# Eight experts' rows scattered to planes of their own, and added to the output on DVE

## What is computed

```
x_flat = layernorm(h).reshape(N, 128)                     # N = 4096
probs  = softmax(x_flat @ Wr, axis=0)
vals, idx = top_k(probs.T, 1024)                          # 8 experts x 1024 rows
g = gelu(x_flat[idx] @ W1[e] + b1[e])                     # 128 -> 512
out_e = g @ W2[e] + b2[e]                                 # 512 -> 128
output = zeros_like(x_flat).at[idx].add(vals * out_e)
result = h + output
```

## Time and profile before

| | |
|---|---|
| median of 3 runs | 872.06 us (868.32 to 873.8) |
| the profiled execution, its own time | 873.6 us |
| its span | 871.7 us |
| PE busy over the span | 675.0 us (77%) |
| DVE busy | 598.2 us (69%) |
| ACT busy | 456.4 us (52%) |
| POOL busy | 201.8 us (23%), of which L517 100.5 us, L504 64.2 us |
| DMA | 23.67 MB, mean 27 GB/s |

### The profile page before, as it was taken

One profiled execution on the slowest core, in us unless ns is written; L12 is line 12 of the kernel. 1 busy time (PEld: TensorE's weight loads), 2 busy tenths in 40 slices (PEclk: granted clock), 3 DMA queues, 4 the chain that ended last, 5 costly groups with the idle time before them and its releaser, 6 DMA issues. The chain is left out here.

```text
span 871.7 us, 12946 instructions
## 1 busy us (share of the span) xinstructions
PE 675.0 (77%) x4060; PEld 447.2 (51%) x4060; DVE 598.2 (69%) x2170; ACT 456.4 (52%) x664; POOL 201.8 (23%) x212
## 2 busy tenths in 40 slices
PE   4687869867999999999999998673323788887380
PEld 2344355455576575575765756452212666664360
DVE  2777797878987979988779689836888455541020
ACT  2967656537867776778677787642001232332020
POOL 1000000001001000010010100001006688888875
PEclk9889988969999999999999998885555899999595
DMA  5200000000000000000000000006001144354333
GB/s 163 84 1 0 2 1 2 0 2 14 2 2 14 2 2 14 2 14 2 2 14 1 2 13 2 14 1 163 0 0 40 46 68 70 76 90 65 39 33 27
DMA packets 34717, 23.67 MB, mean 27 GB/s; under 512 B 8232, under 2 KB 31226, under 8 KB 34628
## 3 DMA queue, kind: packets, MB, share of 16 engines
q0 software_dynamic: 11264, 8.40, 7.1%
q1 hardware_dynamic: 23152, 14.21, 5.8%
q10 hardware_dynamic: 212, 0.08, 0.1%
HBM read 14.29 MB, written 8.39 MB: 26 GB/s over the span
## 5 line engine op out<-in xcount | busy, mean ns | idle before, releaser
L549 ACT ACTIVATE front<-ps 128x1024 f32<-128x1024 f32 x128 | 127.7, 1027 | 37.4 <-PE ps L796 12.8
L646 ACT ACTIVATE front<-front,minus_tau 128x256 f32<-128x256 f32 x256 | 108.6, 497 | 37.6 <-DVE minus_tau L1191 36.5
L549 ACT ACTIVATE back<-ps 128x1024 f32<-128x1024 f32 x72 | 73.7, 1024 | 94.4 <-PE ps L926 82.0
L517 POOL DMA_INDIRECT out_dram<-back x64 | 100.5, 1570 | 23.8 <-issue 22.6
L455 POOL CROSS_LANE_REDUCE more_all<-more 128x1 int32<-128x1 f32 x32 | 11.5, 358 | 398.4 <-DVEq L1116 265.3
L829 PE MATMUL ps<-ident,front 128*128 128x128 f32 x512 | 75.0, 295 | 30.0 <-ACTq L648 21.6
L829 PEld LDWEIGHTS ps<-ident,front 128*128 128x128 f32 x512 | 63.3, 151 | 52.6 <-ACTq L648 31.7
L549 ACT ACTIVATE back<-ps,back 128x1024 f32<-128x1024 f32 x32 | 35.6, 1113 | 103.1 <-PE ps L940 103.1
L504 POOL DMA_INDIRECT back<-rows,back x64 | 64.2, 1003 | 69.6 <-issue 66.9
L954 PE MATMUL ps<-back 128*128 128x128 f32 x512 | 67.6, 300 | 6.0 <-ACT back L549 4.5
L845 PE MATMUL ps<-back,front 128*64 128x256 f32 x512 | 70.8, 408 | 1.2 <-ACT back L549 1.2
(11 more groups left out here) (190 smaller groups left out, 1082.8 us busy)
## 6 DMA issues: line engine op xcount, KB each, us to landing
back<-in_L_ffn_W_dram SPq DMA_DIRECT2D x16, 256.0 KB, 3.4
front<-in_x_dram SPq DMA_DIRECT2D x4, 750.0 KB, 4.5
rows<-xn SPq DMA_DIRECT2D x8, 256.0 KB, 2.2
out_dram<-h SPq DMA_DIRECT2D x1, 2048.0 KB, 7.8
back<-rows,back POOLq DMA_INDIRECT x64, 2.5
out_dram<-back POOLq DMA_INDIRECT x64, 3.3
wqkv<-in_L_attn_W_qkv_dram SPq DMA_DIRECT2D x1, 768.0 KB, 5.7
back<-in_L_ffn_b_dram SPq DMA_DIRECT2D x8, 64.0 KB, 3.7
```

The costliest lines, as they stand in the source:

```text
L517: g.indirect_dma_start(orow[:, :], bass.IndirectOffsetOnAxis(ap=add_at[p][:, s:s + 1], axis=0), y[p][:, s, :], None, compute_op=ALU.add)\
L549: a.activation(dst, ps[s][:, 0:cols], func, **kw).then_inc(sems[f"free{s}"], 1)
L646: a.activation(prob[n % 2][:, r, :], sc[n][:, r, :], ACT.Relu, bias=minus_tau[:, n // 2, n % 2 * 4 + r:n % 2 * 4 + r + 1])
```

## The change

- Device memory gets eight planes of 4096 rows (2 MB each), `plane[e]`. They are zeroed early: POOL clears the tile `hid` (first instruction of its stream, 128x2048), SP stores it twice into `plane[0]` between its second and third load of audio, and later copies `plane[0]` to the seven others, device memory to device memory. ACT waits for `plane0_in` before it first writes to `hid`.
- `scatter(e)` writes plainly to `plane[e]`, with no addition. It no longer waits for scatter(e - 1) at its start; the wait for that stands in its middle, in front of its fifth transfer, and `y_free` is raised there.
- The store of `h` to `out` at the start of the stage is gone. SP loads each plane, when its scatter has landed, into one of three new tiles `z` (2 MB, 128x4096, cut from `front`).
- DVE adds each loaded plane to `h` (`add_plane`, a TENSOR_TENSOR of two SBUF tensors of 128x4096): planes 0, 1 and 2 after the loop over experts, plane 3 after `weighted(5)`, plane 4 after `weighted(6)`, planes 5 and 6 after `weighted(7)`, plane 7 in four quarters.
- SP stores `h` to `out` at the very end, in four quarters, each when DVE has added it.
- The loops of SP and POOL over experts are written out.

```diff
@@ gpsimd
+            g.memset(hid[:, 0:4, :], 0.0).then_inc(sems["hid_zero"], 1)
             g.memset(ident[:, :], 0.0)
...
-            def scatter(e, p, first=False):
+            def scatter(e):
+                p = e % 2
                 g.wait_ge(sems["y_ok"], e * 2 + 1)
-                if not first:
-                    g.wait_ge(sems["y_out"], e * (16 * CT))
-                g.sem_inc(sems["y_free"], 1)
+                g.sem_inc(sems["pool_held"], 1)
                 for s in range(CT):
                     if s == CT // 2:
+                        if e:
+                            g.wait_ge(sems[f"y_out{1 - p}"], ((e - 1) // 2 + 1) * (16 * CT))
+                            g.sem_inc(sems["y_free"], 1)
                         g.wait_ge(sems["y_ok"], e * 2 + 2)
                         g.sem_inc(sems["pool_held"], 1)
-                    g.indirect_dma_start(orow[:, :], bass.IndirectOffsetOnAxis(ap=add_at[p][:, s:s + 1], axis=0),
-                                         y[p][:, s, :], None, compute_op=ALU.add)\
-                        .then_inc(sems["y_out"], 16)
+                    g.indirect_dma_start(plane[e][:, :], bass.IndirectOffsetOnAxis(ap=add_at[p][:, s:s + 1], axis=0),
+                                         y[p][:, s, :], None).then_inc(sems[f"y_out{p}"], 16)
...
+            g.sem_inc(sems["y_free"], 2)
             for e in range(4):
                 gather(e, e % 2)
...
+            g.wait_ge(sems["planes_in"], 16 * (E - 1))
@@ sync
+            sp.wait_ge(sems["hid_zero"], 1)
+            for i in range(2):
+                sp.dma_start(plane[0][i * (NTOK // 2):(i + 1) * (NTOK // 2), :].rearrange("(p j) d -> p j d", p=P),
+                             hid[:, 0:4, :].rearrange("p m (j d) -> p (m j) d", d=D)).then_inc(sems["plane0_in"], 16)
             part_in(2)
...
+            sp.wait_ge(sems["plane0_in"], 32)
+            for e in range(1, E):
+                sp.dma_start(plane[e][:, :], plane[0][:, :]).then_inc(sems["planes_in"], 16)
...
-            sp.dma_start(out.rearrange("b s d -> (b s) d").rearrange("(j p) d -> p j d", p=P),
-                         h[:, :, :]).then_inc(sems["rows_out"], 16)
...
+            for e in range(2):
+                weights_in(e)
+            for e in range(E - 1):
+                if e + 2 < E:
+                    weights_in(e + 2)
+                scattered(e)
+                if e >= NZ:
+                    sp.wait_ge(sems["z_used"], e - NZ + 1)
+                sp.dma_start(z[e % NZ][:, :, :], plane[e].rearrange("(j p) d -> p j d", p=P))\
+                    .then_inc(sems[f"z_in{e % NZ}"], 16)
+            scattered(E - 1)
+            sp.wait_ge(sems["z_used"], E - NZ)
+            last = plane[E - 1].rearrange("(j p) d -> p j d", p=P)
+            for q in range(4):
+                rows = slice(q * NT // 4, (q + 1) * NT // 4)
+                sp.dma_start(z[(E - 1) % NZ][:, rows, :], last[:, rows, :]).then_inc(sems[f"zq_in{q}"], 16)
+            for q in range(4):
+                rows = slice(q * NT // 4, (q + 1) * NT // 4)
+                sp.wait_ge(sems["z_used"], E - 1 + (q + 1))
+                sp.dma_start(orow[:, rows, :], h[:, rows, :]).then_inc(sems["out_ok"], 16)
+            sp.wait_ge(sems["out_ok"], 64)
@@ vector
+            def add_plane(e):
+                v.wait_ge(sems[f"z_in{e % NZ}"], (e // NZ + 1) * 16)
+                v.sem_inc(sems["held"], 1)
+                v.tensor_tensor(h[:, :, :], h[:, :, :], z[e % NZ][:, :, :], ALU.add).then_inc(sems["z_used"], 1)
+                v.drain()
+
+            for e in range(3):
+                add_plane(e)
             for e in range(E - 3, E):
                 weighted(e // 2, e % 2)
+                add_plane(e - 2)
+            add_plane(E - 2)
```

More of the change, by code:

```diff
@@ L163, in audio_tower @@
     rows2 = nc.dram_tensor("rows2", (NTOK, D), f32, kind="Internal").ap()
+    plane = [nc.dram_tensor(f"plane{e}", (NTOK, D), f32, kind="Internal").ap() for e in range(E)]
     ctx = ExitStack()
@@ L317, in audio_tower @@
         slot_i = cut([P, E, CT], i32)
+        NZ = 3
+        z = [cut([P, NT, D]) for i in range(NZ)]
         cut = back()
@@ L422, in _, with weights_in @@
-            sp.wait_ge(sems["y_out"], 16 * E * CT)
+            orow = out.rearrange("b s d -> (b s) d").rearrange("(j p) d -> p j d", p=P)
+            def weights_in(e):
+                p = e % 2
+                sp.wait_ge(sems["ew_used"], e + 1)
+                sp.dma_start(ew1[p][:, :], e_w1[e, :, :]).then_inc(sems[f"ew_in{p}"], 16)
+                sp.dma_start(ew2[p][:, :, :], e_w2[e, :, :].rearrange("(k f) d -> f k d", f=P))\
+                    .then_inc(sems[f"ew_in{p}"], 16)
+                sp.dma_start(eb1[p][:, :], e_b1[e, :].rearrange("(k f) -> f k", f=P),
+                             allow_slow_non_contiguous=True).then_inc(sems[f"ew_in{p}"], 16)
+                sp.dma_start(eb2[p][:, :], e_b2[e, :].partition_broadcast(P)).then_inc(sems[f"ew_in{p}"], 16)
@@ new lines, in scattered @@
+            def scattered(e):
+                sp.wait_ge(sems[f"y_out{e % 2}"], (e // 2 + 1) * (16 * CT))
+            for e in range(2):
[8 more added lines that the diff above has]
+                    .then_inc(sems[f"z_in{e % NZ}"], 16)
@@ L494, in _ @@
             g.engine_nop().then_inc(sems["vals_ok"], 1)
-            g.wait_ge(sems["rows_out"], 16 * (G + 1) + 1)
-            orow = out.rearrange("b s d -> (b s) d")
+            g.wait_ge(sems["rows_out"], 16 * G + 1)
             def gather(e, p, half=range(CT)):
@@ L506, in gather @@
                         .then_inc(sems[f"xg_in{p}"], 16)
[L508 removed]
+            def scatter(e):
+                p = e % 2
                 g.wait_ge(sems["y_ok"], e * 2 + 1)
[L510 to L512 removed]
+                g.sem_inc(sems["pool_held"], 1)
                 for s in range(CT):
                     if s == CT // 2:
+                        if e:
+                            g.wait_ge(sems[f"y_out{1 - p}"], ((e - 1) // 2 + 1) * (16 * CT))
+                            g.sem_inc(sems["y_free"], 1)
                         g.wait_ge(sems["y_ok"], e * 2 + 2)
                         g.sem_inc(sems["pool_held"], 1)
[L517 to L521 removed]
+                    g.indirect_dma_start(plane[e][:, :], bass.IndirectOffsetOnAxis(ap=add_at[p][:, s:s + 1], axis=0),
+                                         y[p][:, s, :], None).then_inc(sems[f"y_out{p}"], 16)
+            g.sem_inc(sems["y_free"], 2)
             for e in range(4):
                 gather(e, e % 2)
[L524 to L530 removed]
+            g.wait_ge(sems["planes_in"], 16 * (E - 1))
+            for e in range(E - 5):
+                scatter(e)
+                gather(e + 4, e % 2)
+            scatter(E - 5)
             gather(E - 1, 1, range(CT // 2))
[L532 removed]
+            scatter(E - 4)
             gather(E - 1, 1, range(CT // 2, CT))
             for e in range(E - 3, E):
[L535 removed]
+                scatter(e)
         @block.scalar
@@ L1491, in _ @@
                 c.leave((E - 4) // 2)
+            def add_plane(e):
[5 more added lines that the diff above has]
+                add_plane(e)
             for e in range(E - 3, E):
                 weighted(e // 2, e % 2)
+                add_plane(e - 2)
+            add_plane(E - 2)
+            for q in range(4):
+                rows = slice(q * NT // 4, (q + 1) * NT // 4)
+                v.wait_ge(sems[f"zq_in{q}"], 16)
+                v.sem_inc(sems["held"], 1)
+                v.tensor_tensor(h[:, rows, :], h[:, rows, :], z[(E - 1) % NZ][:, rows, :], ALU.add)\
+                    .then_inc(sems["z_used"], 1)
 _INS = ['x', 'L0_tok_w1', 'L0_tok_b1', 'L0_tok_w2', 'L0_tok_b2', 'L0_attn_W_qkv', 'L0_attn_W_out', 'L0_attn_b_out',
```

27 lines of the change are left out of this document (4 added, 23 removed).

## The result

The changed kernel took 877.36 us (median of 20 runs, 870.91 to 879.2), the kernel before beside it 871.86 (20 runs, 866.13 to 874.37). The ratio is 1.0051, 95% interval 1.0031 to 1.0071. That lies within the 1% that the prediction put down as hard to tell from no change; the interval leaves out 1 all the same, so the difference is small but real, and it has the other sign than the 869 that was forecast.

A forecast was written before the change was run, and what follows sets the result against it. POOL's time per indirect transfer, then the tail behind expert 7's rows, was taken as the bound. Scatters landing 15.0 us sooner, less 10.5 of longer tail and 1 for start and weights, gave 3.5 sooner: 869 us, range 853 to 884.

The forecast's parts named there:

- the landing of gather 7: Expert stage: second half starts at 801.8, last transfer at 805.5 lands 2.5 us later, at 808.0; PE waits about 6.5 us.
- POOL's timetable: POOL's gathers and scatters: pairs of 20.4 us from 701.0 keep PE's pace, so scatter 4 starts at 777.5.
- the tail: After scatter 7 lands: plane 7 loaded, added and stored, 13.6 us against 3.1 before, 10.5 more.
- The price of a plain scatter: POOL's scatters: without addition 0.94 us each like a gather, instead of 1.55, saving 5.1 us an expert.
- Rival (B): POOL's scatters: 1.55 us is the price of any scatter, not its addition; slower, 888 us; chance 0.18.
- The holds: POOL transfers started inside a 4.45 us DVE addition stand until it ends, one transfer per addition instead of 3.6.
- Rival (A): POOL beside DVE's additions: not held, or only slightly; 852 us, about 860 with half the hold; chance 0.29 together.
- an addition might stand behind a running transfer: DVE's additions: by the skill page each could begin up to 0.94 us later, 1 to 2 us in sum; left out.
- Scatter 7: POOL's last scatter: held in the additions of planes 5 and 6, last transfer starts at 851.0, landed at 853.6.
- The start and expert 6's weights: Early zeroing, and weights queued behind plane 3 on SP: 0 to 2 us each, 1 us put for both.
- rival (C): Start phase or expert stage: seven copies or eight 2 MB loads hold up other transfers by 5 to 10 us; 878; chance 0.08.

The follow-up runs named there:

- e4: The kernel before with the addition taken out of its scatters and nothing else changed (expert sum left out): 839.11 us, ratio 0.9645.
- e1: The changed kernel with the seven whole-plane additions cut to 8 columns each, loads and waits kept: 854.38 us, ratio 0.9822.
- e3: The changed kernel with each whole-plane addition split into 8 instructions of 128x512, nothing left out: 858.01 us, ratio 0.9874.
- e2: The changed kernel with loads of planes 0 to 6 cut to 64 KB, POOL clearing the z tiles first, additions whole: 873.71 us, ratio 1.0053.
- f3: The changed kernel with the load of plane 4 alone cut to one group of 128 rows: ratio 1.0373, in the slower condition.
- g1: The changed kernel with only plane 4's load cut to one group of 128 rows, run again: ratio 1.0386, in the slower condition.
- e6: The kernel before with only the early zeroing of the planes added, planes unused: 878.83 us beside 877.76, ratio 1.0001.
- e11: The changed kernel with each of the seven whole additions replaced by a one-operand pass of 128x4096: 866.03 us, ratio 0.9956.
- f1: The changed kernel once more, nothing altered, in the slower condition: 913.76 us beside 880.42 for the kernel before, ratio 1.0382.

## Why the prediction was wrong

Forecast 3.5 us sooner, measured 5.5 later: 9 us off, all in one direction. The mechanism was right; three terms of the sum were too small. The largest is the landing of gather 7, for which the sum took 2.5 us behind POOL's last transfer, from rows with no 2 MB load beside it, and which measured 6.8 beside the load of plane 4. The others are POOL's timetable, in which holds by VectorE's short products stood at nothing and measured 2.9 us, and the tail, 13.6 us forecast and 15.6 measured. By the prediction's own steps, with the changed kernel's times shifted by 3.9:

- **The price of a plain scatter.** Forecast 0.94 from the gather; measured 0.97. Rival (B) falls. e4 shows the saving by itself, 30 us.
- **The holds.** Forecast: a transfer started inside an addition stands until it ends, one transfer per addition. Measured so, seven of them at 4.1 to 4.9 us. The additions took 4.42 (forecast 4.45). Rival (A), no hold, is what e1 and e3 make of it: its 852 stands beside their 854.4 and 858.0. The prediction also left out that an addition might stand behind a running transfer, and that was right: none did. Its row for it was read loosely, since in the earlier trace rows VectorE's product starts 0.04 us ahead of the scatter of 706.75, not with it; the addition of 780.59, begun beside a running transfer, is the clearer one.
- **POOL's timetable.** Scatter 4 began at 780.2, forecast 777.5: +2.7. It is the holds by VectorE's short products in the loop, which the earlier trace rows had shown and the timetable left out: five scatters took 1.13 to 2.02 us, 2.9 more together than at 0.97. The price has no part in it, for the timetable had put 10.2 us for eight transfers, and eight plain scatters without a hold took 10.2 (805.29 to 815.51).
- **The landing of gather 7.** Its second half began at 804.1, forecast 801.8, so the arithmetic of the holds was right within 0.4 us. But its last transfer landed 6.8 us after its start, not 2.5, beside the load of plane 4, which the step on gather 7 had not put there. Expert 7's first layer began at 827.4, forecast 820.5, and its rows were complete at 844.9, forecast 838.0: +6.9, of which about 4 from this. That the load delays the landing is shown by e2's profile (2.6 us). That it reaches the end is shown by e2 in part: its expert stage is 5.3 us shorter and its tail the same, but its median shows it only after the estimated 3.6 us of its clearing are taken off. It cuts seven loads at once, and f3 and g1, which were meant to settle the one load, ran in the other condition.
- **Scatter 7.** Last start 858.0, forecast 851.0: +7.0, passed on.
- **The tail.** Forecast 13.6 us behind the landing, measured 15.6. A quarter (512 KB) took 6.0 us to load, and its store 4.9 where a straight line between two store rows had given 3.0.
- **The start and expert 6's weights.** 1 us was set aside. The clearing costs nothing (e6); the weights made TensorE wait 1.9 us, hidden by the longer wait for gather 7. With the holds gone the same queueing cost 3.25 us (e3). That is -1.

The sum: 2.7 + 4.2 + 2 - 1 = 7.9 of the 9; the last 1 us is within the scatter of the medians.

The measured time lay inside the range of 853 to 884 and beside rival (C), which had said 878. That closeness is partly luck. (C) had the seven copies or the eight loads hold up other transfers by 5 to 10 us; the copies cost nothing, the loads some 4 us in the stage, and the rest is the short holds and the tail. Still, the loads should have been a term of the sum: they had no row, and each other term that rested on a landing had its row from a stretch without them.

## What to carry to other kernels

When work moves from one engine to another, ask first what the new instruction holds while it runs. Here a saving of 30 us on POOL was more than spent: 15 us on loading, adding and storing the planes, most of it in the tail, and 20 on seven VectorE instructions of 4.4 us that held POOL. The same additions in pieces of 0.6 us gave 15 of the 20 back (ratio 1.005 to 0.987). Then ask of each landing time in the sum which transfers will be in flight beside it after the change, and what now stands behind the new transfers on their queue. When an experiment cuts something out, check what its own helper instructions cost: the clearing in e2 hid 4 us. And where a comparison's kernel before is itself several us off its usual time, compare nothing across; a condition that cost the kernel before 1% cost the one with less slack 4%.

## What the runs showed of the hardware

- A scatter of 128 rows costs POOL 0.97 us without addition, 1.55 with, and a gather 0.94.
- A VectorE instruction over 128x4096 holds every POOL transfer started inside it, with two operands (such transfers took 4.1 to 4.9 us) and with one (2.4 to 2.9); with two, a transfer already begun runs on, with one it is held as well (e11).
- Beside back-to-back pieces of 128x512 a POOL transfer takes 1.50 us instead of 0.97, about one for every three pieces.
- The other way round, clearing 128x4096 on POOL, three times in a row (10.5 us), made a VectorE copy of 128x32 take 2.82 us instead of 0.18 (e2).
- A 2 MB load from device memory into 128 partitions in rows of 512 bytes lands after 10.8 us (median of seven), and the last part of gather 7 beside it after 6.8 instead of 2.5; SyncE's next issue right behind such a load takes 4.8 to 5.8 us (planes 3 and 4).
- In some comparisons TensorE's signals reach VectorE and ScalarE late while POOL's transfers complete, in every kernel profiled there: at the three experts looked at 8.0, 9.5 and 5.9 us with plain scatters (f1), 6.4, 2.8 and 4.2 with adding ones (e6). Why is open.
